# Mixture of experts: the routing's weights reach the experts' rows through DRAM and broadcast DMAs instead of a TensorE product

## The reference, cut to what matters

```python
logits = x @ gate_w.T                              # 4096 tokens x 16 experts
probs = softmax(logits)
rw, sel = top_k(probs, 2)
rw = rw / rw.sum(axis=-1, keepdims=True)
combine = zeros((N, 16)).at[arange(N)[:, None], sel].set(rw)
gu = einsum('nd,edf->nef', x, w_gate_up)           # 16 experts, 128 -> 2 x 64
g, h = split(gu, 2, axis=-1)
h = silu(g) * h
expert_out = einsum('nef,efd,ne->nd', h, w_down, combine)
shared = silu(x @ shared_w_gate.T) * (x @ shared_w_up.T) @ shared_w_down.T   # width 352
shared = shared * sigmoid(x @ shared_gate_w.T)
out = expert_out + shared
```

## Time and profile before

| what | value |
|---|---|
| median of 3 runs | 2449.13 us (2446.01 to 2450.11) |
| the profiled execution's own time | 2443.93 us |
| its span, first to last instruction | 2441.8 us |
| mean granted TensorE clock | 0.918 of full |
| PE, DVE, ACT, POOL busy | 82%, 74%, 59%, 37% of the span |
| first layer norm work of the MoE stage | from about 2137 us |
| first product of the expert loop | 2206.4 us |

### The profile page before, as it was taken

The page is one execution under the profiler, slowest core; times in us unless marked ns, Lnnn a source line. Parts: engine busy times, 40 slices in busy tenths (PEclk is TensorE's granted clock), DMA queues, the critical chain, the costliest instruction groups (busy, mean ns, idle before and its releaser), DMA issues. The chain is left out here.

```text
span 2441.8 us, 55893 instructions
## 1 busy us (share of the span) xinstructions
PE 2011.8 (82%) x15622; PEld 1555.8 (64%) x15622; DVE 1809.6 (74%) x5679; ACT 1440.6 (59%) x3917; POOL 910.1 (37%) x1342
## 2 busy tenths in 40 slices
PE   3799999999999999984340359999999989959997
PEld 2688888888888888872230137777777756526665
DVE  5788888888888888865667737887878778854554
ACT  3455555555555555555265438878887878744443
POOL 2433333333333333312133303333333347634554
PEclk8799999999999999996575669999999999969999
DMA  4211111111111111000000012222222200010001
GB/s 133 62 32 31 30 30 30 30 30 30 30 30 30 30 30 30 17 1 0 0 0 0 0 42 65 65 61 69 67 62 60 65 1 1 1 26 1 1 0 34
DMA packets 113673, 77.03 MB, mean 32 GB/s; under 512 B 12385, under 2 KB 99777, under 8 KB 113473
## 3 DMA queue, kind: packets, MB, share of 16 engines
q1 hardware_dynamic: 112086, 73.99, 11.4%
q10 hardware_dynamic: 1194, 1.58, 0.2%
q0 software_dynamic: 320, 0.60, 0.1%
HBM read 71.67 MB, written 4.46 MB: 31 GB/s over the span
## 5 line engine op out<-in xcount | busy, mean ns | idle before, releaser
L758 ACT ACTIVATE a_prob<-a_neg,a_nmax 128x289 f32<-128x289 f32 x512 | 269.9, 529 | 172.7 <-DVE a_nmax L684 170.8
L1636 ACT ACTIVATE b_prob<-b_neg,b_nmax 128x257 f32<-128x257 f32 x512 | 255.6, 505 | 98.0 <-DVE b_nmax L1586 97.9
L650 POOL TENSOR_TENSOR a_xn<-a_z,g 128x256 f32<-128x256 f32 x128 | 93.0, 727 | 585.8 <-DVE a_z L714 585.8
L803 PE MATMUL a_score<-a_xnT,a_qT 128*128 128x290 f32 x1536 | 274.1, 314 | 33.3 <-DVE a_qT L738 32.6
L830 PE MATMUL a_out<-a_probT,a_xn 128*128 128x256 f32 x1024 | 269.6, 386 | 0.3 <-DVE a_probT L699 0.3
L803 PEld LDWEIGHTS a_score<-a_xnT,a_qT 128*128 128x128 f32 x1536 | 215.5, 190 | 85.3 <-issue 76.7
L729 DVE TENSOR_SCALAR a_prob<-a_prob,a_rinv 128x256 f32<-128x256 f32 x512 | 256.8, 561 | 4.5
L684 DVE CUSTOM_DVE_ANT_0 a_neg<-a_score,a_bias 128x289 f32<-128x289 f32 x512 | 216.6, 454 | 40.3 <-PE a_score L803 36.4
L1586 DVE CUSTOM_DVE_ANT_0 b_neg<-b_score,b_bias 128x257 f32<-128x257 f32 x512 | 195.9, 421 | 32.1 <-PE b_score L1678 32.1
L830 PEld LDWEIGHTS a_out<-a_probT,a_xn 128*128 128x128 f32 x1024 | 175.6, 190 | 21.0 <-DVE a_probT L699 3.8
L2338 POOL TENSOR_TENSOR m_hidden<-m_full,m_hidden 128x512 fp32r<-128x512 f32 (+1 forms) x88 | 113.6, 1292 | 129.0 <-ACT m_hidden L2319 129.0
(11 more groups left out here) (472 smaller groups left out, 5259.6 us busy)
## 6 DMA issues: line engine op xcount, KB each, us to landing
a_raw<-in_ctx SPq DMA_DIRECT2D x128, 128.0 KB, 3.3
b_raw<-in_ctx SPq DMA_DIRECT2D x128, 128.0 KB, 3.2
a_kept<-keep SPq DMA_DIRECT2D x32, 257.0 KB, 3.9
b_kept<-keep SPq DMA_DIRECT2D x32, 257.0 KB, 3.6
b_v_rows<-ctx_tail_values SPq DMA_DIRECT2D x32, 256.0 KB, 3.5
a_tail<-latents_normalised SPq DMA_DIRECT2D x64, 64.0 KB
latents_normalised<-lat_affine SPq DMA_DIRECT2D x8, 256.0 KB, 2.3
out<-x SPq DMA_DIRECT2D x1, 2048.0 KB
```

The costliest lines, as they stand in the source:

```text
L758: nc.scalar.activation(prob[:, par, grp, :], neg[:, grp, :], ACT.Exp, bias=nmax[:, par, grp:grp + 1], scale=-1.0, accum_out=rsum[:, par, g ...
L803: last = nc.tensor.matmul(score_ps[grp % 2][:, 0:even(KEYS0)], qT[:, a, un, bn, 4 * grp:4 * grp + 4, :], xnT[:, c, n, :], start=(p == 0), ...
L1636: nc.scalar.activation(prob[:, n, grp, :], neg[:, par, grp, :], ACT.Exp, bias=nmax[:, par, grp:grp + 1], scale=-1.0, accum_out=rsum[:, n, ...
```

## The change

The selector, its load, its copy and the product `m_wide` are gone, and so are the bf16 parts. Block 3 of the routing turns `first` itself (16 columns of f32), ScalarE copies each chunk to one of two small buffers, and SP stores it to a DRAM tensor of 16 x 4096 f32. In the expert loop SP loads, for each expert item, two rows of that tensor, each broadcast over 64 partitions, into one of four buffers `m_wide` in SBUF, and VectorE multiplies by that.

```diff
@@ moe_routing, block 2
-                nc.vector.tensor_tensor(first[:], first[:], second[:], ALU.add).then_inc(chain, 1)
-                dve.wait_ge(chain, n + 6)
-                n += 6
-                for part in range(PARTS):
-                    nc.vector.tensor_copy(parts[:, :, part, :], first[:]).then_inc(chain, 1)
...
+                nc.vector.tensor_tensor(first[:], first[:], second[:], ALU.add).then_inc(comb_ready, 1)
+                dve.wait_ge(comb_ready, 1)
@@ moe_routing, block 3
-            @block.vector
-            def _(dve):
...
-                        nc.vector.tensor_copy(comb[:, u], parts[:, ds((c + u) * GRP, GRP), :, :].rearrange("p t n e -> p t (n e)"))\
-                            .then_inc(staged, 1)
...
+                for c in range(CHUNKS):
+                    pe.wait_ge(comb_copied, c + 1)
+                    for j in range(GRP):
+                        last = nc.tensor.transpose(comb_ps[c % 2][0:E_N, j * P:(j + 1) * P], first[:, c * GRP + j, :], k.ident[:])
+                    last.then_inc(comb_turned, 1)
...
+                        act.wait_ge(comb_turned, c + (u + 1))
+                        act.wait_ge(comb_stored[u], g * 16 + 16)
+                        nc.scalar.activation(combT[:, u, :], comb_ps[u][0:E_N, :], ACT.Copy).then_inc(comb_copied, 1)
...
+                        sp.wait_ge(comb_copied, c + (u + 3))
+                        sp.dma_start(k.comb_dram[:, ds((c + u) * CH, CH)], combT[:, u, :]).then_inc(comb_stored[u], 16)
+                for u in range(2):
+                    sp.wait_ge(comb_stored[u], CHUNKS // 2 * 16 + 16)
@@ moe1
+        wide = sb("m_wide", [P, 4, CH])
...
+            @block.sync
+            def _(sp):
+                def chunk(c):
+                    for j in range(PAIRS):
+
+                        if j >= 4:
+                            sp.wait_ge(full_ready, c * ITEMS + (j - 3))
+                        else:
+                            wait(sp, full_ready, (c - 1) * ITEMS + (j + 5))
+                        for e in range(2):
+                            sp.dma_start(wide[e * E_FF:(e + 1) * E_FF, j % 4, :],
+                                         k.comb_dram[2 * j + e:2 * j + e + 1, ds(c * CH, CH)].broadcast_to([E_FF, CH]))\
+                                .then_inc(wide_loaded[j % 4], 16)
...
-                        nc.tensor.matmul(wide_ps[:], k.pair_select[:, j, :], combT[:, ds(c * CH, CH)], start=True, stop=True)\
-                            .then_inc(wide_done, 1)
...
-                            dve.wait_ge(wide_done, c * PAIRS + (j + 1))
+                            dve.wait_ge(wide_loaded[j % 4], c * 64 + (j // 4 + 1) * 32)
                             wait(dve, lo_ready, n - 1)
-                            nc.vector.tensor_tensor(full[:, u, :], gated[:], wide_ps[:], ALU.mult).then_inc(full_ready, 1)
-                            dve.wait_ge(full_ready, n + 1)
-                            dve.sem_inc(wide_used, 1)
+                            nc.vector.tensor_tensor(full[:, u, :], gated[:], wide[:, j % 4, :], ALU.mult).then_inc(full_ready, 1)
```

More of the change, by code:

```diff
@@ L52 @@
 PAIRS = E_N // 2
-PARTS = 3
 SH_FF = 352
@@ L1977, in product, with moe_routing @@
     return last
-def moe_routing(k, yT, y, combT, share, sh_row, weights, loads):
+def moe_routing(k, yT, y, share, sh_row, weights, loads):
     nc = k.nc
@@ L2064, in _ @@
                 dve.wait_ge(gathered, CHUNKS + 2)
-        chain, ratio_ready, share_done, share_ready = (sem(f"mr_{n}") for n in ("chain", "ratio_ready", "share_done", "share_ready"))
+        chain, ratio_ready, share_done, share_ready, comb_ready = (
+            sem(f"mr_{n}") for n in ("chain", "ratio_ready", "share_done", "share_ready", "comb_ready"))
         with nc.Block() as block:
@@ L2140, in _ @@
                 pool.wait_ge(w_lo, len(weights))
-        staged, comb_turned, comb_copied = sem("mr_staged"), sem("mr_comb_turned"), sem("mr_comb_copied")
+        comb_turned, comb_copied = sem("mr_comb_turned"), sem("mr_comb_copied")
+        comb_stored = [sem(f"mr_comb_stored{u}") for u in range(2)]
         with nc.Block() as block:
-            @block.vector
-            def _(dve):
[L2146 to L2149, removed]
-                        nc.vector.tensor_copy(comb[:, u], parts[:, ds((c + u) * GRP, GRP), :, :].rearrange("p t n e -> p t (n e)"))\
-                            .then_inc(staged, 1)
             @block.tensor
             def _(pe):
[L2155 to L2163, removed]
+                pe.wait_ge(comb_ready, 1)
+                for c in range(CHUNKS):
[3 more added lines that the diff above has]
+                    last.then_inc(comb_turned, 1)
             @block.scalar
@@ L2170, in _ @@
                     for u in range(2):
-                        act.wait_ge(comb_turned, c + (u + 3))
-                        nc.scalar.activation(combT[:, ds((c + u) * CH, CH)], comb_ps[u][0:PARTS * E_N, :], ACT.Copy).then_inc(comb_copied, 1)
-                act.wait_ge(comb_copied, CHUNKS + 2)
+                        act.wait_ge(comb_turned, c + (u + 1))
[4 more added lines that the diff above has]
+                for u in range(2):
+                    sp.sem_inc(comb_stored[u], 16)
+                with sp.Fori(0, CHUNKS // 2) as g:
+                    c = g * 2
+                    for u in range(2):
+                        sp.wait_ge(comb_copied, c + (u + 3))
+                        sp.dma_start(k.comb_dram[:, ds((c + u) * CH, CH)], combT[:, u, :]).then_inc(comb_stored[u], 16)
+                for u in range(2):
+                    sp.wait_ge(comb_stored[u], CHUNKS // 2 * 16 + 16)
 def moe1(k, io):
@@ L2198, in moe1 @@
             gate_up = io["L1_ffn_w_gate_up"].rearrange("e d f -> d e f")
-            moe_routing(k, yT, y, combT, share, sh_row, [
+            moe_routing(k, yT, y, share, sh_row, [
                 (sh_row, k.sh_gate_row[:]),
@@ L2208, in moe1 @@
         act_in, mul_in = ([psum(f"m_{n}{u}") for u in range(2)] for n in ("g", "h"))
-        wide_ps, expert_ps, shared_ps, turn_ps = (psum(f"m_{n}") for n in ("wide", "expert", "shared", "turn"))
+        expert_ps, shared_ps, turn_ps = (psum(f"m_{n}") for n in ("expert", "shared", "turn"))
+        wide = sb("m_wide", [P, 4, CH])
         silu, gated, full = sb("m_silu", [P, 2, CH]), sb("m_gated", [P, CH]), sb("m_full", [P, 2, CH])
@@ L2247, in moe1, with _ @@
         with nc.Block() as block:
+            @block.sync
+            def _(sp):
+                def chunk(c):
[8 more added lines that the diff above has]
+                                .then_inc(wide_loaded[j % 4], 16)
+                chunk(0)
+                with sp.Fori(1, CHUNKS) as c:
+                    chunk(c)
             @block.tensor
```

25 lines of the change are left out of this document (6 added, 19 removed).

## The result

| | before | after |
|---|---|---|
| median, 20 runs each | 2447.28 us (2445.21 to 2450.43) | 2451.73 us (2449.79 to 2453.92) |
| ratio | 1 | 1.0017, 95% interval 1.0011 to 1.0023 |
| profiled execution's span | 2441.8 us | 2448.9 us |
| VectorE busy, share of span | 74% | 76% |

The change costs 4.45 us (interval 2.7 to 5.6): slower, as forecast, by half of the forecast 8.8. It is 0.18% of the time, under the 0.2% from which the prediction counted a change as slower; to a time within 0.2% it gave a chance of 0.27. The profiled spans differ by 7.1 us. I set stage against stage before reading single rows; times are from the first instruction.

What follows compares the result with a forecast made beforehand. TensorE was taken to bound the expert loop; setup -0.6, block 2 0, block 3 +6.7, entry +1.1 and +0.7, loop +0.9 sum to +8.8 us on 2449.13, forecast 2458 us, own range 2452 to 2466.

Steps and rivals of the forecast that it cites:

- The bound and the loop: Expert loop: TensorE bound before; after, m_full and GpSimd's low half exclude each other, 2.61 us per item, +0.9 us with drain.
- Rival (b): Expert loop: no exclusion, TensorE sets 2.07 us per item, a chunk takes 23.3 us, total 2424 us; chance 0.10.
- Rival (a): Expert loop: VectorE gets in before GpSimd, items alternate, a chunk takes 26.09 us, total 2446 us; chance 0.24.
- The drain: End of the expert loop's chunks: the last items drain in the locked cycle, about +0.7 us.
- Block 3: Routing: ScalarE's copies wait until the small buffers are stored, 2.99 us a round; +6.7 us, bounds 0 to +10.3.
- Entry: Start of the expert loop: first m_full waits for its load, +1.1 us, and TensorE's clock is low, +0.7.
- half clock: Loop's entry: after transposes alone TensorE's granted clock is 0.50 for 4.1 us; +0.7 us, between 0 and 2.
- Setup: Setup: VectorE's copy of the selector, ahead of the quantisation TensorE waits on, goes; -0.6 us, bounds 0 to -1.2.
- Base: Whole kernel: the sum of +8.8 us was added to a median of 2449.13 us.
- block 2: Routing: the 2.8 us of VectorE's splitting that goes are covered by ScalarE's last gate; 0 us.

Runs made afterwards that it cites:

- e1: Changed kernel with m_gated in the freed PSUM bank, so m_full has one operand in SBUF instead of two: 2423.59 us, ratio 0.9894 to before.
- e3: Changed kernel with four semaphore increments ahead of GpSimd's low half to put it off: 2453.76 us, ratio 1.0025 to before.
- e7: Changed kernel with the four loads of the loop's first two items issued in block 3, behind stores: 2450.21 us, ratio 1.0016 to before.
- e6: Kernel before with the 128 loads added into buffers nothing reads, m_full waiting for them but still reading PSUM: 2447.20 us, ratio 1.0004.
- all four repairs: Changed kernel with m_gated in PSUM, block 3's copies in one tile, early first loads and added TensorE products in block 3: 2420.72 us, ratio 0.9892.
- e5: Kernel before, product m_wide kept, but m_full reads a tile in SBUF instead of the product's PSUM bank: 2459.65 us, ratio 1.0055.
- e8: Changed kernel with products into a bank nothing reads, to keep TensorE busy in block 3: 2449.96 us, ratio 1.0012 to before.
- the two repairs: Changed kernel with m_gated in PSUM and block 3's copies in one tile, waiting for no store: 2418.21 us, ratio 0.9888 to before.

## Why the prediction was right and wrong

- **The bound and the loop: right.** A chunk of 27.49 us was forecast, 27.47 measured (the kernel before has 27.57, so 0.1 less and not 0.03 more), for the reason given: `m_full` and the low half exclude each other (e1: -28 us without it), and GpSimd is first, here by 0.11 and not in a tie. The high half starts 0.04 behind `m_full` instead of the 0.07 of the earlier trace rows, so the circle is 2.57 where 2.61 stood. Rival (b) was priced at 2424 if there were no exclusion; e1, which has none, took 2423.6, in part by luck: its chunk is 24.05 and not 23.3, which over eight chunks is 6 us, and block 3 and the base were lower than in that sum. Rival (a)'s mechanism exists (e3), but its time couldn't be had by putting GpSimd off.
- **The drain: wrong sign.** +0.7 was added for items that drain in the locked cycle; from the seventh to the last addition to `x` it is 15.94 against 16.73, -0.8.
- **Block 3: right mechanism, wrong size; this is the step that failed.** The prediction took "the 2.3 us of the eight stores to DRAM, the nearest row", but those stores are of 256 KB and these of 32 KB. They land in 1.6, a round is 2.3 to 2.4 instead of 2.99, and the block grew by 4.44 instead of 6.7. Put into the prediction's own sum, 1.6 for each of the four landings takes off 2.8 us and gives +3.9; the other 0.5 lies mostly in the last round, where ScalarE's second copy starts 0.86 us behind the first, and behind the last copy (2.77 us to the first product). The bounds allowed for it (0 to +10.3). That the smaller size is the reason is likely and not shown: no run changed it alone, and in the earlier trace rows a DMA of 64 KB took 3.2 us, longer than the stores of 256.
- **Entry: nearly the right sum, wrong parts.** The first `m_full` is 1.3 us later where 1.8 was forecast. Load and clock were added, but they lie beside each other: with the load early it is still 1.1 late (e7), with the clock up in the kernel before it is 1.0 late from the load alone (e6). The half clock itself came as forecast: by the means of 0.50 and 0.61 above it ends at about 2216.3, some 3.9 us into the loop where 4.1 stood.

By the Trainium skill, "TensorE: Matmul & The Clock Gate", Part 4 (PE-mode transpose), transposes don't count as activity to the clock gate, and the prediction read from it that the half clock at the entry was certain. The traces agree for this kernel (0.50 ahead of the loop) and not throughout: in the kernel before, block 3 holds only transposes too, and the clock stayed at 1.00.

- **The first chunk.** From the first `m_full` to the first addition to `x` are 40.94 us instead of 39.72, +1.2, which no step had; six chunks at 27.47 give 0.6 back. Neither load nor clock makes it: with the load early it is 40.98 (e7), and without the exclusion it is 34.60 at half clock (e1) and 34.51 at full clock (all four repairs). It is the exclusion once more: in the kernel before the ends of the first three `m_full` lie 1.75 and 1.91 us apart, since TensorE has no down products to make yet, in the changed kernel 2.60 and 2.57, the locked circle from the first item on. The lags were carried through a chunk in the middle and not through the first. With the entry's 1.3 and the drain's -0.8 the loop costs the 1.14 of the trace, where 2.7 had been forecast.
- **Setup: 0 instead of -0.6.** The copy's time is saved and absorbed by 1461 us. A stage that starts earlier isn't yet a gain.
- **The range.** Added up, the bounds named for block 3, the clock and the lags reach from 2449.8 to 2463.7; the 2452 to 2466 written beside them does not follow from them, and 2451.73 lies just under it.
- **Base.** The sum was put on a median of 3 runs, 2449.13; 20 runs give 2447.28. Of the miss of 6.3 us 1.9 is that, and 4.4 the sum.

Terms in order (setup, block 2, block 3, entry and loop): forecast -0.6, 0, 6.7, 2.7; read from the trace 0, -0.2, 4.4, 1.1, together 5.4, inside the interval of the measured 4.45 (without the 1.7 us ahead of block 2). So a product of 0.5 us per item was taken from TensorE, and nothing came of it, because in exchange `m_full` lost its PSUM operand. Neither part shows this by itself: the exclusion costs 12.6 us with the product in place (e5) and 28.1 without it (e1 against after).

## What to carry to other kernels

Before an intermediate is moved from PSUM to SBUF, see which engine reads it and whether GpSimd works beside it on SBUF operands. Here a VectorE product that kept one operand in PSUM was untouched (0.69 us in all 64 items of e1), one with both in SBUF waited until GpSimd's instruction was done (1.72), and that cost 28 us. When a bank is freed, try the other operand there. Price a DMA from a row that is alike in size and shape as well as in direction, or give the term the whole spread of such rows. Where two delays start together, take the longer and not the sum: here 1.1 and 1.0 us gave 1.3. And carry the lags through the first items too.

## What the runs showed of the hardware that I had not expected

- The exclusion is a matter of 0.03 us in the starts: GpSimd ahead by that much runs its 1.28 and VectorE takes 1.80; VectorE ahead by 0.14 runs its 0.69 and GpSimd takes 1.69 (e3). With one VectorE operand in PSUM 63 of the 64 overlap GpSimd's instruction in the kernel before and in e1 and take 0.69.
- 128 loads of 128 KB, each one row spread over 64 partitions, at 75 GB/s beside a loop whose engines work in SBUF, slowed no instruction measurably (e6).
- In e8 TensorE ran products until 2209.25, was idle for 2.04, and the granted clock was still 1.00 for the loop's first `m_g` (0.93 us for three passes); it fell in the `m_h` behind it, under back to back products. So it was with the two repairs, where block 3 holds transposes alone and TensorE was idle for 3.50 us: 0.93 us for the first `m_g`, 1.42 for the `m_h` behind it. In the kernel with all four, after 2.34 us idle, it did not fall. What decides between them stays open.
